# Twelve matmuls without a result in two of TensorE's waits at the start of the width-one attention

## What is computed

```python
x = x + _L1_xattn_ref(_layernorm(x), ctx_1024, ctx_1024, ...)
x = x + _L1_ffn_ref(_layernorm(x), ...)        # fp8 matrix product
x = x + _L2_attn_ref(_layernorm(x), L2_attn_w_qkv, L2_attn_w_out)

def _L2_attn_ref(x, w_qkv, w_out):              # 64 heads, each of width one
    qkv = jnp.einsum('bnc,fc->bnf', x, w_qkv)
    ...
    dots = jnp.einsum('bhid,bhjd->bhij', q, k) * scale
    dots = jnp.where(causal, dots, -jnp.inf)
    attn = jax.nn.softmax(dots, axis=-1)
    out = jnp.einsum('bhij,bhjd->bhid', attn, v)
    ...
    return jnp.einsum('bnh,ch->bnc', out, w_out)
```

## Time and profile before

| | us |
|---|---|
| runs without the profiler | 3162.99, 3165.30, 3179.05 (median 3165.3) |
| the profiled execution, its own time | 3160.37 |
| its span, first to last instruction | 3158.4 |
| mean granted clock of TensorE over the span | 0.969 |
| TensorE busy | 2935.1 (93%) |
| VectorE busy | 1863.5 (59%) |
| ScalarE busy | 1254.6 (40%) |

### The profile page before, as it was taken

How to read it: one execution, slowest core, us unless ns; L and a number is a source line. 1 busy time by engine, 2 the same in 40 slices (tenths; PEclk the granted TensorE clock), 3 DMA queues, 4 the chain that set the end, 5 groups by cost and what they waited for, 6 DMA issues and landing times.

```text
span 3158.4 us, 52225 instructions
## 1 busy us (share of the span) xinstructions
PE 2935.1 (93%) x20631; PEld 1955.1 (62%) x20671; DVE 1863.5 (59%) x6438; ACT 1254.6 (40%) x1944; POOL 431.8 (14%) x458
## 2 busy tenths in 40 slices
PE   7999999988989889988998999999999999998998
PEld 4666666865555556655665556566667766766653
DVE  5534443699999536875678787574244344434455
ACT  2222222335656433324443578554332333323443
POOL 0010010114343311000000256300000000000000
PEclk9999999999999999999999799899999999998999
DMA  3000000010000000000000011100000000000000
GB/s 129 1 1 0 1 1 1 1 53 1 2 1 2 34 33 1 1 2 4 2 1 5 24 36 28 42 1 27 1 1 0 1 1 1 0 1 9 2 1 27
DMA packets 22028, 37.75 MB, mean 12 GB/s; under 512 B 2132, under 2 KB 19733, under 8 KB 20760
## 3 DMA queue, kind: packets, MB, share of 16 engines
q1 hardware_dynamic: 20968, 34.02, 3.2%
q10 hardware_dynamic: 816, 0.39, 0.1%
HBM read 26.81 MB, written 2.10 MB: 9 GB/s over the span
## 4 chain that ended last, share of the span: by engine, by line
PE 77%; DVE 17%; ACT 4%; issue 2%; DMA 0%; DVEq 0%; SPq 0%; POOL 0%; ACTq 0%; POOLq 0%
PE ps L415 45%; DVE arena L568 3%; PE ps L620 2%; PE ps L688 2%; PE ps L3053 2%; PE ps L3072 2%; ACT arena L674 2%; PE ps L1603 2%; PE ps L2369 2%; PE ps L2323 2%; PE ps L516 2%; DVE arena L1937 2%; PE ps L729 2%; PE ps L2926 1%; PE ps L553 1%
## 5 line engine op out<-in xcount | busy, mean ns | idle before, releaser
L415 PE MATMUL ps<-weights,arena 128*128 128x256 f32 (+4 forms) x2480 | 692.2, 428 | 43.1 <-DVE arena L1818 26.1
L415 PEld LDWEIGHTS ps<-weights,arena 128*128 128x128 f32 (+1 forms) x2480 | 460.8, 195 | 209.9 <-issue 93.7
L415 PE MATMUL ps<-arena,weights 128*128 128x256 f32 (+4 forms) x1726 | 560.8, 473 | 13.7 <-DMA weights<-in_w_L_attn 5.8
L415 PEld LDWEIGHTS ps<-arena,weights 128*128 128x128 f32 (+1 forms) x1726 | 316.2, 191 | 217.7 <-issue 157.4
L415 PE MATMUL ps<-arena 128*128 128x256 f32 (+4 forms) x1618 | 426.2, 416 | 6.0 <-ACT arena L4771 1.5
L415 PEld LDWEIGHTS ps<-arena 128*128 128x128 f32 (+2 forms) x1618 | 298.0, 188 | 115.0 <-issue 74.9
L568 DVE TENSOR_REDUCE arena<-ps 128x16 f32<-128x1232 f32 (+2 forms) x96 | 179.1, 1865 | 150.6 <-PE ps L546 51.7
L674 ACT ACTIVATE arena<-ps 77x2048 f32<-77x2048 f32 (+1 forms) x112 | 210.1, 1876 | 124.6 <-PE ps L620 62.8
L1937 DVE MATCH_REPLACE8 arena<-arena 128x77 f32<-128x77 f32 x1024 | 214.3, 224 | 0.0
L2336 ACT ACTIVATE arena<-ps 128x1536 f32<-128x1536 f32 x128 | 185.7, 1452 | 57.4 <-PE ps L2325 50.5
L857 POOL TENSOR_TENSOR x<-x,weights 128x512 f32<-128x512 f32 x32 | 43.9, 1372 | 1195.2 <-DVE arena L823 1148.6
(11 more groups left out here) (427 smaller groups left out, 4432.7 us busy)
## 6 DMA issues: line engine op xcount, KB each, us to landing
arena<-arena SPq DMA_DIRECT2D x156, 32.0 KB
weights<-in_w_L_ffn SPq DMA_DIRECT2D x1, 3848.0 KB, 11.5
weights<-in_w_L_attn SPq DMA_DIRECT2D x1, 3840.0 KB, 15.0
weights<-in_w_L_xattn SPq DMA_DIRECT2D x3, 1024.0 KB, 6.3
weights<-in_w_L_ffn SPq DMA_DIRECT2D x1, 3072.0 KB, 10.5
x<-in_x SPq DMA_DIRECT2D x2, 1024.0 KB
weights<-in_w_L_xattn SPq DMA_DIRECT2D x1, 2048.0 KB, 7.4
out<-x SPq DMA_DIRECT2D x8, 256.0 KB, 2.2
```

Source lines behind the costliest of these rows:

```text
L415: ins = k.nc.tensor.matmul(out, lhsT, rhs, start=start and i == 0, stop=i == n - 1)
```

## The change

A function `awake_tensor` issues n f32 matmuls of 128 x 128 on 512 columns of `ctxT` into one bank of PSUM. Nothing reads them. The next real matmul into the bank starts it anew. There are two calls in batch 0: 7 matmuls into bank 3 between the wait for `v` and the wait for the row transfers, and 5 matmuls into bank 0 at g = 2, between the scores of group 2 and the wait for "o". The second call has a wait of its own, for the probabilities of groups 0 and 1, since ScalarE reads bank 0 for group 1.

```diff
--- before.py
+++ after.py
@@ -729,6 +729,12 @@
             ins = k.nc.tensor.transpose(out[:, (2 * c + t) * P:(2 * c + t + 1) * P], src[:, t, c * P:(c + 1) * P],
                                         k.ident[:, :])
     return ins
+
+
+def awake_tensor(k, b, n):
+
+    for _ in range(n):
+        k.nc.tensor.matmul(k.ps[:, b, :], k.ctxT[:, 0, 0:P], k.ctxT[:, 0, 0:512], start=True, stop=True)
 
 
 def flat(tile):
@@ -2427,6 +2433,7 @@
         for g in range(GROUPS):
             if n == 0 and g == 0:
                 pe.wait_ge(*s.sig.at("v", 0, 0, 1))
+                awake_tensor(k, 3, 7)
             if n == 0 and g == 1:
                 after(pe, x, left, "raw", 2)
                 pe.wait_ge(*x.sig.at("f_scaled", 0, B - 3, 1))
@@ -2443,6 +2450,8 @@
             if n == 0 and g == 0:
                 pair_back_tensor(k, pe, x, left, 6)
             if n == 0 and g == 2:
+                pe.wait_ge(*s.sig.at("prob", 0, 0, 2))
+                awake_tensor(k, 0, 5)
                 after(pe, x, left, "o")
                 fp8_turn_tensor(k, pe, x, older, 7)
             if n == 0 and g == 3:
```

## The result

The two kernels were run alternately on the same chip, 22 times each. The kernel before has a median of 3163.05 us (3160.08 to 3182.32), the changed one 3179.61 (3161.21 to 3185.69). The ratio is 1.0028, 95% interval 1.0015 to 1.0041, so about 9 us slower. The means are 3166.4 and 3175.2 us.

A forecast was written before the change was run, and what follows sets the result against it. TensorE, 77% of the chain, was taken to bound the kernel, with other engines limiting gains; 6.1 - 0.45 - 2.3 + 0 = 3.35 or 3.4 us, put on the median of four, gave 3167.5 us, range 3157.5 to 3178.

The forecast's parts named there:

- Price of the calls: At the two calls: seven matmuls are 14 records in 6.6 us, five are 10 records in 4.7 us.
- The rival with one record for a matmul: At the two calls: a matmul is one record, calls take 3.3 and 2.4 us, about 3158 us; chance 0.03.
- Steps 1 to 4: From first call to turn: both calls overrun their waits, turn starts 6.1 us late, L1081 behind it 5.65 late.
- Step 5: Groups 3 to 5: VectorE limits, TensorE waits 3 us for the copy, full clock gives back 2.3 us.
- Step 6: At L415: the clock halves after the 3 us wait, L415 takes 3.6 us and ends 3.4 us late.
- The clock falls in spite of the fill: Between the calls: clock falls, second call costs 9.3 us and not 4.7; +10.7 us, 3171 us; chance 0.1.
- Faster: Start of batch 1: wait on L2345 shortens, the low clock behind it goes; 3157.5 to 3159.3 us; chance 0.15.
- The sum, +3.4: Whole kernel: 6.1 - 0.45 - 2.3 + 0 = 3.35, or 3.4 us with rounding, giving 3163.8 us profiled.
- Behind L415 both kernels are alike: After L415: both kernels run alike at full clock, VectorE moves along with TensorE, so the delay stays 3.4 us.
- the low clock lasts beyond L415: Groups 7 to 10 run at half clock because the rise after L415 doesn't come; about +13 us, 3173; chance 0.12.

The follow-up runs named there:

- third fill: Three more matmuls in the wait for the copy of the turned mean, against the changed kernel; ratio 1.0050 to the kernel before, all 12 executions above 3173.
- the larger set: Changed kernel unaltered, all sessions, beside the kernel before: 28 of 58 executions against 27 of 97 above 3173 us.
- the one matmul: One matmul in the wait for the first mean, added to kernel before, changed kernel, third fill: medians 3165.2, 3165.7, 3167.5 us; none above 3173.
- the short calls: One matmul and two in place of seven and five, against the changed kernel; median 3160.3 us, ratio 0.9990 to the kernel before.

## Why the prediction was right, and where not

- *Price of the calls*: right. 6.3 and 4.6 us for 6.6 and 4.7. The rival with one record for a matmul is out: 14 and 10 records.
- *Steps 1 to 4*: right, the turn 5.4 us late where 6.1 were forecast; the difference is the records' length and the exp of group 1, which came sooner.
- *Step 5*: right, with luck in the number. The full clock gave back 2.2 us and VectorE's copy became the limit; TensorE waits 3.6 us for it (3 forecast). VectorE's chain began 0.8 us sooner than forecast, counted from the fp8 product, and took 6.7 us and not 6.1: L2584 took 0.73 us and L2598 1.39, where the same work (L2575, L2589) took 0.42 and 0.95 before. The two misses nearly cancel.
- *Step 6*: right. The clock fell in that wait and L415 took 3.68 us. The third fill shows the cause: filled, 1.99 us. The prediction says that a rule on keeping TensorE busy speaks against this step; as it is put there it speaks for it, since the third wait is one with nothing in it.
- *The clock falls in spite of the fill*: didn't happen, in none of four profiles. The rule of the Trainium skill that transposes don't count as activity for the clock ("TensorE: Matmul & The Clock Gate", Part 4, PE-mode transpose) did not bring the rival about as I weighed it: the clock was 1.00 over eight transposes and the groups of 32 rows around them. That doesn't refute the rule, since the eight take 1.10 us, no longer than the idle wait of 1.16 us over which the clock held too.
- *Faster*: didn't happen. The wait at the start of batch 1 is 1.8 us (1.7 before), and the low clock behind it lasts 20.5 us in both profiles.
- *The sum, +3.4*: right for the stretch (+3.15) and for the lower group (+3.4 +- 1.5).
- *"Behind L415 both kernels are alike"*: this is the step that failed. It holds for two profiles, which run side by side at a distance of 9.4 us from group 7 to the end. It doesn't hold for the set of executions. 58 us behind the change stands a wait of 1.2 us at which the clock sometimes falls, at a price of about 16 us, and more executions of the changed kernel lie above 3173. The groups' means are 3162.4 and 3177.0 before, 3165.4 and 3182.0 after, 14.6 and 16.6 us apart; 0.32 more of the executions x 16 is 5.1 us of the 8.8 between the means, and 3.2 are the stretch; by the larger set the share is 0.20 and its part 3.2 us. The rival *the low clock lasts beyond L415* didn't happen in any of the four profiles of the changed kernel. With the second call alone it did, for 20.5 us and at a price of 8.1; in the changed kernel the loss lies at the wait for the first mean, as the runs with the one matmul show. The scatter of the three runs (3163 to 3179), which I took for noise, was most likely this.

That the wait for the first mean makes the upper group is shown by the one matmul in it, three kernels over. Why the changed kernel falls there more often isn't settled. The profiles give a hint only: from the last rise of the clock to the start of that wait it is 8.8 to 9.0 us in the seven profiles where the clock held (the kernel before, four of the changed kernel, the first call alone, the short calls), and 8.6 us in the two where it fell (the third fill, the second call alone). Whether and how a shift of 3 us at the entry changes that distance in the unprofiled executions no run shows.

## What to carry to other kernels

Work put into a wait must fit it: count the records of one matmul in the trace first (two for f32), and remember that the wait of one engine may be the head start of another. Here 11.3 us were put into less than 4, and the higher clock could return only what the next engine had in reserve, 2.2 us. Work that fits isn't enough either: the short calls let TensorE reach the next wait sooner, and the clock fell there. Where a kernel's times lie in two groups, find the wait that makes them before costing anything of a few us: a short wait on which the clock hangs can be worth more than the change under study.

## What wasn't expected of the hardware

- A single wait of 1.17 us was followed by 37.5 us at half clock, and the same wait of 1.16 to 1.17 us by none in seven other profiles.
- With one full f32 matmul in the first wait the clock held there and fell 4 us behind it, in the next wait (2.0 us); it rose again 1.3 us behind four f32 records at half clock (3.8 us).
- The profiled executions of the two kernels are 6.3 us apart ahead of the change, in stages where their instructions are the same, and those of the changed kernel alone by up to 8.3 us.
